# Two attention layers of a four-block transformer kernel: scores contracted over the 32 channels of four heads, on a 32-row strip of the array, instead of over all 128

## What is computed

```python
# block 2 (layer 4)
q = (x @ Wq.T).reshape(B, LQ, 16, 8).transpose(0, 2, 1, 3)
kv = (y @ Wkv.T).reshape(B, LK, 16, 16).transpose(0, 2, 1, 3)
k, v = jnp.split(kv, 2, axis=-1)
q, k = _rope(q), _rope(k)
probs = jax.nn.softmax(jnp.einsum('bhqd,bhkd->bhqk', q, k), axis=-1)
out = jnp.einsum('bhqk,bhkd->bhqd', probs, v)
# block 3 (layer 6): no rope, biases on q, k, v, a mask over the keys,
# scores times 8 ** -0.5, otherwise the same
```

## Time and profile before

| | us |
|---|---|
| median of 3 runs | 1663.77 |
| lowest and highest | 1659.76, 1664.92 |
| span of the profiled execution | 1655.4 |
| TensorE matmul busy | 1534.5 (93%) |
| TensorE weight loads busy | 1230.4 (74%) |
| VectorE busy | 872.3 (53%) |
| ScalarE busy | 768.8 (46%) |
| GpSimd busy | 105.0 (6%) |

### The profile page before, as it was taken

The page is one execution under the profiler, slowest core; times in us unless marked ns, Lnnn a source line. Parts: engine busy times, 40 slices in busy tenths (PEclk is TensorE's granted clock), DMA queues, the critical chain, the costliest instruction groups (busy, mean ns, idle before and its releaser), DMA issues.

```text
span 1655.4 us, 27913 instructions
## 1 busy us (share of the span) xinstructions
PE 1534.5 (93%) x9596; PEld 1230.4 (74%) x9596; DVE 872.3 (53%) x2194; ACT 768.8 (46%) x1662; POOL 105.0 (6%) x99
## 2 busy tenths in 40 slices
PE   4899899999999988999968989999999999788999
PEld 2697477777899765779947965677778987567798
DVE  6763455565333846743367625555644347466432
ACT  2743354445443454454446424554554434535353
POOL 1021000000000001000011210000000000010000
PEclk8999999999999998999989999999999999999799
DMA  4002000000000200000000020000000020000000
GB/s 179 1 2 94 10 1 1 1 1 1 1 1 1 103 1 1 5 1 14 2 15 1 1 102 0 1 2 1 1 1 1 1 99 5 1 1 2 1 8 7
DMA packets 3499, 27.74 MB, mean 17 GB/s; under 512 B 510, under 2 KB 1048, under 8 KB 2336
## 3 DMA queue, kind: packets, MB, share of 16 engines
q1 hardware_dynamic: 2496, 19.42, 3.0%
q10 hardware_dynamic: 864, 6.48, 1.0%
HBM read 24.84 MB, written 1.05 MB: 16 GB/s over the span
## 4 chain that ended last, share of the span: by engine, by line
issue 82%; PE 10%; POOL 6%; DVE 1%; DMA 0%; ACT 0%; POOLq 0%; SPq 0%; DVEq 0%; ACTq 0%
PE psum L642 9%; POOL probs L1186 2%; POOL rs L1151 2%; POOL arenaD L1168 1%; PE psum L645 1%; DMA mask<-in_mask_dram 0%; DVE nmax L1297 0%; DVE psum L1293 0%; ACT arenaA L959 0%; DVE xn L1244 0%; POOL mmv L1180 0%; POOL probs L1162 0%; POOL moe L1162 0%; POOL arenaA L1160 0%; ACT probs L959 0%
## 5 line engine op out<-in xcount | busy, mean ns | idle before, releaser
L642 PEld LDWEIGHTS psum<-moe,arenaA 128*128 128x128 f32 x2048 | 240.0, 195 | 6.1 <-ACT arenaA L959 1.5
L642 PE MATMUL psum<-moe,arenaA 128*128 128x128 f32 x2048 | 242.7, 278 | 1.0 <-ACT xnT L959 1.0
L959 ACT ACTIVATE arenaB<-psum 128x512 f32<-128x512 f32 x448 | 169.8, 432 | 140.9 <-PE psum L645 140.9
L959 ACT ACTIVATE probs<-psum,nmax 128x589 f32<-128x589 f32 (+1 forms) x256 | 125.7, 554 | 165.2 <-DVE nmax L1366 161.0
L959 ACT ACTIVATE arenaA<-psum,vec 128x512 f32<-128x512 f32 (+1 forms) x208 | 125.3, 613 | 147.2 <-PE psum L642 146.5
L1345 DVE SCALAR_TENSOR_TENSOR x<-psum,gt,x 128x128 f32<-128x128 f32 x256 | 72.1, 344 | 217.5 <-PE psum L642 217.5
L642 PE MATMUL psum<-parts 128*128 128x512 f32 x672 | 166.8, 398 | 0.0
L645 PE MATMUL psum<-w_first,probs 128*128 128x128 f32 (+2 forms) x1120 | 160.9, 275 | 3.1 <-ACT arenaA L959 3.1
L1366 DVE TENSOR_REDUCE nmax<-psum 128x1 f32<-128x589 f32 x128 | 98.7, 771 | 119.8 <-PE psum L642 119.5
L645 PEld LDWEIGHTS psum<-w_first,probs 128*128 128x128 f32 (+2 forms) x1120 | 131.8, 144 | 24.9 <-issue 16.9
L642 PEld LDWEIGHTS psum<-parts 128*128 128x128 f32 x672 | 122.4, 188 | 23.7
(11 more groups left out here) (194 smaller groups left out, 2281.4 us busy)
## 6 DMA issues: line engine op xcount, KB each, us to landing
moe<-in_w_moe_dram SPq DMA_DIRECT2D x4, 4096.0 KB, 12.8
w_l<-in_w_l_dram ACTq DMA_DIRECT2D x1, 2048.0 KB, 9.5
w_l<-in_w_l_dram ACTq DMA_DIRECT2D x1, 1372.0 KB, 12.3
x<-in_x_dram SPq DMA_DIRECT2D x4, 256.0 KB, 4.2
w_second<-in_w_second_dram ACTq DMA_DIRECT2D x1, 1024.0 KB, 8.4
w_rest<-in_w_rest_dram ACTq DMA_DIRECT2D x1, 1024.0 KB, 5.0
out_dram<-x SPq DMA_DIRECT2D x4, 256.0 KB, 2.1
w_first<-in_w_first_dram ACTq DMA_DIRECT2D x1, 596.0 KB, 5.8
```

Source lines behind the costliest of these rows:

```text
L642: return nc.tensor.matmul(out, lhsT, rhs, start=start, stop=stop)
L959: return nc.scalar.activation(out, in_, func, **kw)
```

## The change

The contraction of the scores in layers 4 and 6 goes over 32 partitions, those of the four heads concerned, instead of 128. For half hf and r the strip begins at partition 32 * (2 * hf + r): 0 and 32 for hf = 0, 64 and 96 for hf = 1. The keys are set out for four heads (308 columns) instead of 16 (1232), since each strip of 32 partitions needs only its own four: `block` has 4 columns, and row p is 1 in column (p mod 32) div 8. GpSimd's multiplication so writes 128x308 elements instead of 128x1232, and the table's group of weights is 6 KB smaller. The order of the instructions on each engine is the same as before, and so is their number.

```diff
-        ("twist", 128), ("cos", 512), ("sin", 512), ("block", 16), ("before", 64), ("gate1", 8)]
+        ("twist", 128), ("cos", 512), ("sin", 512), ("block", 4), ("before", 64), ("gate1", 8)]
...
-        kbd = [arenaD[:, 1280 * s:1280 * s + 16 * KEYS].rearrange("p (h k) -> p h k", h=16) for s in range(NS)]
+        kbd = [arenaD[:, 320 * s:320 * s + 4 * KEYS].rearrange("p (j k) -> p j k", j=4) for s in range(NS)]
...
-                        h = 4 * (2 * hf + r)
-                        last = mm(slot(i, 4 * KEYS, at=512 * r), rot[s][:, 0, t * 128:(t + 1) * 128],
-                                  kbd[s][:, h:h + 4, :].rearrange("p j k -> p (j k)"))
+                        strip = slice(32 * (2 * hf + r), 32 * (2 * hf + r) + 32)
+                        last = mm(slot(i, 4 * KEYS, at=512 * r), rot[s][strip, 0, t * 128:(t + 1) * 128],
+                                  kbd[s][strip, :, :].rearrange("p j k -> p (j k)"))
...
-                nc.gpsimd.tensor_tensor(kbd[s], rot[s][:, 1, 0:KEYS].unsqueeze(1).broadcast_to([128, 16, KEYS]),
-                                        W["block"].unsqueeze(2).broadcast_to([128, 16, KEYS]), ALU.mult)\
+                nc.gpsimd.tensor_tensor(kbd[s], rot[s][:, 1, 0:KEYS].unsqueeze(1).broadcast_to([128, 4, KEYS]),
+                                        W["block"].unsqueeze(2).broadcast_to([128, 4, KEYS]), ALU.mult)\
                     .then_inc(*heads_ready.mark(l, s))
...
-    block = (heads[:, None] // 8 == _np.arange(16)[None, :]).astype(_np.float32)
+    block = (heads[:, None] % 32 // 8 == _np.arange(4)[None, :]).astype(_np.float32)
```

## The result

| | before | changed |
|---|---|---|
| median of 5 runs, us | 1663.77 | 1713.87 |
| lowest and highest | 1657.68, 1665.17 | 1704.17, 1715.25 |
| span of the profiled execution | 1655.4 | 1702.4 |

The changed kernel is slower: the ratio of the times is 1.032 (95% interval 1.028 to 1.037). Forecast were 1672.2 us, between 1659 and 1687; the sign was right, the size was wrong. Its time lies 1.8 us above its span, and every other run that has both numbers shows about the same. So of the 8.4 us between the span and the median before, most is the spread between executions and not what lies around a span.

A forecast was written before the change was run, and what follows sets the result against it. TensorE was taken as the bound in layer 4, a chain over VectorE in layer 6. Parts 1 to 4 gave -0.4 us, clock falls +8.8: span 1663.8, plus 8.4 to the median, 1672.2 us, range 1659 to 1687.

The forecast's parts named there:

- Part 1: TensorE entering and leaving strips at each unit's scores: two changes cost 0.40 us, 0.20 in and 0.20 out.
- Part 2: Scores on two strips: only the middle two records overlap, 0.26 us less; net +0.14 us a unit on TensorE.
- rival C: Scores: whole second matmul runs beside the first and the clock stays; -9.7 us, 1654.1 us; chance 0.11.
- Part 3: What counts of the net: layer 4 +2.8 us on 20 TensorE-paced units, layer 6 -1.0 us on the VectorE chain.
- Part 4: Keys on GpSimd: 0.69 us for 308 elements, TensorE's 1.12 us wait in layer 4 gone, -2.2 us over both passes.
- Part 5: Layers 4 and 6: thin matmuls hold TensorE's clock less; six falls to half clock at 1.46 us each, +8.8 us.
- A: Clock doesn't mind thin matmuls, overlap as in part 2; parts 1 to 4 alone, 1663.4 us, no change; chance 0.28.
- B: Scores: no overlap of strips at all; +10.1 us, 1673.9, or 1682.7 with clock falls; chance 0.19 with or without falls.
- D: The slice makes no difference to the array: neither changes nor overlap, only GpSimd's part, 1661.6 us; chance 0.06.

The follow-up runs named there:

- one_strip: Changed kernel with both matmuls of a unit on the same 32-row strip, so nothing runs side by side: 1773.64 us (a single time).
- small_table: Changed kernel with scores over all 128 rows again, keeping GpSimd's table of four heads: 1655.51 us, ratio 1.000 to the kernel before.
- rows_65: As small_table, but scores over partitions 0 to 64 in the full array, without strips: 1714.89 us (a single time).
- filled_more: Changed kernel plus two unread full-row matmuls of 384 columns in each turning of heads and output projection of layer 6: 1680.18 us (a single time).
- filled: Changed kernel plus one unread full-row matmul of 256 columns in each turning of heads and output projection of layer 6: 1734.62 us, ratio 1.043.

## Why the prediction was wrong

**Part 1** (0.40 us for going in and out) held where TensorE had no wait: one_strip, with strips and no overlap, takes 0.38 us more for one unit of layer 4. For the next it takes only 0.11 more. There the kernel before had a gap on TensorE, which now hides a part: behind the turning of heads the first mixing record started 0.26 us later, and starts 0.16 us later with strips. So a unit pays 0.25 us on average, not 0.40.

**Part 2** (overlap of 0.26 us, "by the order") was wrong in my favour. The order of issue doesn't hold the second strip back: its first record starts 6 ns beside the first strip's first, ahead of the first strip's second. (The bias matmul below shows the same by names.) The four records start within 0.37 us in place of one_strip's 0.88: the overlap is 0.51 us, the bound of 0.52 and not 0.26. This is rival C's mechanism. The net is -0.13 us for a unit without a wait (2.88 to 2.75), C's -0.12, and -0.16 on average, not +0.14. Here the Trainium skill's rule that I cited, that matmuls of different row groups run together but start in program order ("TensorE: Matmul & The Clock Gate", Part 3), is borne out in the running together (starts 6 ns apart) and not in the order.

**Part 3** follows: layer 4's body gives about 20 x 0.16 = 3.2 us instead of costing 2.8. Layer 6's chain over VectorE, from which I had -1.0, no longer sets anything, since TensorE at half clock never waits.

**Part 4** held: L1168 takes 0.70 us (0.69 forecast), the wait is gone, and it gives 1.18 us a pass in small_table (1.1 forecast).

**Part 5** is the step that failed, by its size. Its sign and its reason (thin matmuls count for less) were right, and the run with 65 rows shows it in layer 6 apart from everything else. Even the six falls came where they were counted: near the four starts, at 542, 644, 1381 and 1490 us, and in the two bodies of layer 6, at 675 and 1518. But I priced a fall as an event that ends by itself after one unit's mixing and transposes, 1.46 us, so +8.8 for six, with +17.5 more as the bound. The trace has 10, 20, 17 and 20 us at half clock for the starts, and 48 us on end for each body, where each unit takes 5.51 us instead of 3.50. In layer 6 the two kinds together cost some 36 us. Page and spans agree on the whole: before, 1655.4 x 0.019 x 2 = 63 us were at half clock, afterwards 1702.4 x 0.066 x 2 = 225. The 162 us more at half clock cost 47 us and not 81, which fits the waits that TensorE had to use up and the gain of the overlap, though no run separates the two. The bound should have been made from a whole sequence at half clock, and the rows for it were there: 7.00 us for two units, TensorE busy for 23.29 of 26, would become 7.00 x 23.29 / 26 x 2 = 12.5 us (11.98 in rows_65), and four such pairs +22 us a pass.

Of the rivals, A fell with the clock. B, run as one_strip, gave not 1682.7 but 1773.64 us, by the same wrong price of the clock in the main. C had the mechanism of the overlap right but not "the clock stays". D fell with the record starts.

What stays open: why layer 4's body holds the full clock with the same strips and the same share of them, and layer 6's doesn't. The two differ in several things at once (bias matmuls of one row, waits for VectorE, the start), which no run separates. Open too is what makes layer 4 fall near its start on strips and not with 65 rows in the full array.

## What to carry to other kernels

A matmul record that contracts over few rows takes as long as one over all 128 (0.26 us for 308 columns on 32, 65 and 128 rows), and counted for less in holding TensorE's clock in layer 6: before narrowing the contraction of a kernel whose TensorE is the bound, price the whole stage at half clock, and look in the trace afterwards whether the clock stays where the narrow matmuls are. Full rows whose entries are mostly zeros, which look like waste, can be what keeps the engine fast: the keys before were zero in 15 of 16 rows of every column, and the clock held. And when TensorE is at half clock and never waits, the granted clock is the first column to read, ahead of any count of instructions.

## What the hardware showed that I had not expected

Matmuls on different strips don't keep their order. Timeline of TensorE, changed kernel, layer 6, where a bias matmul stands right ahead of a unit's scores, both on strips:
```profile
672.18 0.37 PE L642 MATMUL psum<-rows,ones 1*128 1x128 f32 x1
672.19 0.52 PE L642 MATMUL psum<-arenaD,qh 32*128 32x308 f32 x1
672.39 0.27 PE L642 MATMUL psum<-rows,ones 1*128 1x128 f32 x1
672.50 0.68 PE L642 MATMUL psum<-arenaD,qh 32*128 32x308 f32 x3
```
A score record starts 14 ns behind the first record of the bias matmul, and 0.2 us before that matmul's second record, which was issued earlier. Singly, the other three score records start at 672.50, 672.56 and 672.77 us, and the one at 672.56 carries the semaphore increment that only the unit's last matmul has: its second strip ran ahead of its first. The completion was not signalled early for that. The increment came at 673.21 us, 0.03 us after the last of the four had ended, as in the other units (0.01 to 0.03), and 0.24 us after the record that carries it.

And time can fall by adding work: filled_more, with 1.3 us of useless matmuls in every unit of layer 6, took 34 us less than the changed kernel without them, on another chip, and 54 us less than filled with a third of them.
